# Attention's filling phase: two bias sums, one score step and the number of identity products moved

## The reference, cut to what matters

```
x = x + 0.5 * ffn(layernorm(x))          # shared SwiGLU plus one of 8 experts per token
x = x + attention(layernorm(x))          # the layer that the change touches
x = x + 0.5 * ffn(layernorm(x))
```

```
k, q, v = x @ Wk, x @ Wq / 4, x @ Wv          (per head)
s1 = softmax(q  @ k_l^T)     512 x 64
s2 = softmax(q_l @ k_l^T)     64 x 64
s3 = softmax(q_l @ k^T)       64 x 512
out = s1 @ (pinv(s2) @ (s3 @ v)) @ Wo + bo     (pinv: 6 steps of an iteration of matmuls)
```

## Time and profile before

| | |
|---|---|
| time, median of 3 runs | 1135.99 us (1130.5 to 1139.51) |
| the profiled execution | 1137.43 us |
| its span | 1135.5 us |
| PE busy | 1096.2 us, 97% of the span |
| DVE busy | 764.8 us, 67% |
| ACT busy | 582.7 us, 51% |
| POOL busy | 550.8 us, 49% |
| mean granted PE clock | 0.992 |
| busy of 46 us from 384 us on | PE 39.55, DVE 34.24, ACT 23.85, POOL 27.54 us, clock 0.93 |
| busy of 330 us from 430 us on | PE 313.21, DVE 258.77, ACT 173.72, POOL 131.49 us, clock 0.99 |

### The profile page before, as it was taken

How to read it: one execution, slowest core, us unless ns; L and a number is a source line. 1 busy time by engine, 2 the same in 40 slices (tenths; PEclk the granted TensorE clock), 3 DMA queues, 4 the chain that set the end, 5 groups by cost and what they waited for, 6 DMA issues and landing times.

```text
span 1135.5 us, 30299 instructions
## 1 busy us (share of the span) xinstructions
PE 1096.2 (97%) x11410; PEld 891.7 (79%) x11411; DVE 764.8 (67%) x1411; ACT 582.7 (51%) x961; POOL 550.8 (49%) x764
## 2 busy tenths in 40 slices
PE   8999999999999889999999999989999999999997
PEld 6788888888888767677777777768888888888886
DVE  5736656767677487868878878755447477677674
ACT  4344336666666345555555555243433256666663
POOL 5720644676666553444543541327202726566664
PEclk8999999999999989999999999999999999999999
DMA  7273134222211220000000000105241232122220
GB/s 259 74 292 117 37 116 173 66 67 71 66 61 45 65 89 3 3 3 3 3 3 3 3 3 3 39 3 212 101 152 38 102 140 68 62 67 62 71 65 14
DMA packets 39472, 80.25 MB, mean 71 GB/s; under 512 B 6452, under 2 KB 31159, under 8 KB 38336
## 3 DMA queue, kind: packets, MB, share of 16 engines
q1 hardware_dynamic: 27568, 52.94, 12.9%
q0 software_dynamic: 11232, 25.20, 7.1%
q10 hardware_dynamic: 560, 0.52, 0.1%
HBM read 57.13 MB, written 27.00 MB: 74 GB/s over the span
## 4 chain that ended last, share of the span: by engine, by line
PE 80%; DVE 11%; ACT 4%; issue 2%; POOL 1%; DMA 1%; ACTq 0%; DVEq 0%; SPq 0%; POOLq 0%
PE PS L1851 19%; PE PS L1765 13%; PE PS L1865 12%; PE PS L1781 8%; PE PS L1858 3%; PE PS L1939 3%; PE PS L1696 2%; DVE A_NM L801 2%; PE PS L2059 2%; PE PS L1799 2%; PE PS L2072 2%; DVE A_NM L808 1%; ACT XNT L1272 1%; PE PS L1792 1%; PE PS L2010 1%
## 5 line engine op out<-in xcount | busy, mean ns | idle before, releaser
L1851 PE MATMUL PS<-WHL,XGH 128*128 128x512 f32 x624 | 217.5, 430 | 0.6 <-DVE WHL L682 0.6
L1865 PE MATMUL PS<-WD,XNT 128*128 x624 | 149.5, 382 | 1.5 <-ACT XNT L1191 1.5
L703 DVE SCALAR_TENSOR_TENSOR XNT<-PS,SCORES,XNT 128x512 f32<-128x512 f32 x78 | 58.6, 751 | 117.4 <-PE PS L1851 117.4
L1599 POOL TENSOR_TENSOR A_W<-A_XC,CB 128x256 f32<-128x256 f32 x86 | 61.7, 737 | 151.4 <-DVE A_XC L906 151.4
L1186 ACT ACTIVATE XNT<-PS,SCORES 128x512 f32<-128x512 f32 x78 | 53.8, 690 | 145.2 <-PE PS L1851 145.0
L1851 PEld LDWEIGHTS PS<-WHL,XGH 128*128 128x128 f32 x624 | 111.4, 189 | 18.8 <-DVE WHL L682 1.1
L1865 PEld LDWEIGHTS PS<-WD,XNT 128*128 128x128 f32 x624 | 112.6, 190 | 15.6 <-issue 2.0
L1506 POOL DMA_INDIRECT X<-xs_dram,WHO x78 | 96.5, 1238 | 57.6 <-issue 23.1
L1851 PE MATMUL PS<-WHL,XGL 128*128 128x512 f32 x312 | 123.2, 395 | 0.0
L1500 POOL TENSOR_SCALAR XNT<-WD 128x128 f32<-128x128 f32 x64 | 52.4, 838 | 128.9 <-DVE WD L576 128.9
L1781 PE MATMUL PS<-SDH,HHL 128*128 128x256 f32 x512 | 104.0, 287 | 1.7 <-DVE X L616 1.3
(11 more groups left out here) (280 smaller groups left out, 2555.1 us busy)
## 6 DMA issues: line engine op xcount, KB each, us to landing
xs_dram<-WG SPq DMA_DIRECT2D x16, 512.0 KB, 3.0
WU<-in_r_up SPq DMA_DIRECT2D x2, 4096.0 KB, 14.3
shared_dram<-X SPq DMA_DIRECT2D x16, 512.0 KB, 2.9
WG<-in_r_gate SPq DMA_DIRECT2D x2, 4096.0 KB, 16.7
WD<-in_r_down SPq DMA_DIRECT2D x4, 2048.0 KB, 8.2
X<-in_x SPq DMA_DIRECT2D x7, 512.0 KB, 9.6
X<-mid_dram SPq DMA_DIRECT2D x7, 512.0 KB, 3.9
X<-xs_dram,WHO POOLq DMA_INDIRECT x78, 3.0
```

What stands on the lines that cost most here:

```text
L703: dve.scalar_tensor_tensor(B["RH"][:, u * F:(u + 1) * F], banks[3 + u][:], score(t), B["RS"][:, u * F:(u + 1) * F], ALU.mult, ALU.mult).th ...
L1599: pool.tensor_tensor(B["W"][:].rearrange("p (a m) -> p a m", m=M)[:, part, :], B["XC"][b % 2][:].rearrange("p (a w) -> p a w", w=XW)[:, pa ...
L1851: ins = pe.matmul(banks[bank][:], tok, w[:, k * F:(k + 1) * F], start=(k == 0 and i == 0), stop=(k == KD - 1 and i == 2))
L1865: ins = pe.matmul(banks[7][:, 0:D], B["HT"][:, u * F + f * P:u * F + (f + 1) * P], B["WD"][:, bass.ds(ex * (KF * D) + f * D, D)], start=(f ...
```

## The change

On POOL, `s2_normalise(0)` moves ahead of the first two bias sums. On PE, 8 in place of 3 identity products stand behind the transposes of batch 1, and the second step of the first softmax's scores stands directly behind the first Q projection of batch 1, ahead of the third softmax's transposed scores.

```diff
@@ attention_pool
             batch_root(1)
             batch_normalise(1)
+            s2_normalise(0)
             add_bias(0)
             add_bias(1)
-            s2_normalise(0)
             batch_root(2)
             batch_normalise(2)
             chain_w(0, 0)
@@ attention_tensor
             turn(1, 0)
             turn(1, 1)
-            fill(1, 3)
+            fill(1, 8)
             pe.wait_ge(att["s3m"], count("s3m", 0, 4))
             turn_nm3(0)
@@
             first_s1_max(0)
             pe.wait_ge(att["xtl"], count("xtl", 1, 2))
             project_qk(1, 0)
+            pe.wait_ge(att["s1m"], count("s1m", 0, 1))
+            first_s1_max(1)
             pe.wait_ge(s_picks, 5)
             pe.wait_ge(att["s2s"], count("s2s", 0, 1))
             s3_turned(0, 0)
-            pe.wait_ge(att["s1m"], count("s1m", 0, 1))
-            first_s1_max(1)
             project_qk(1, 1)
             pe.wait_ge(att["s1m"], count("s1m", 0, 2))
             first_s1_max(2)
```

## The result

The change makes the kernel a little slower: 1139.53 us (median of 20 runs) against 1134.26 for the kernel before (20 runs), a ratio of 1.0045 with an interval (here and below of 95%) from 1.0033 to 1.0057, or 5.1 us. The forecast was 1133.5 us and a gain of 2.45: wrong in its sign, and the time lies 1.5 us above its range. The profiled execution after took 1140.97 us, with a span of 1139.0.

What follows compares the result with a forecast made beforehand. Bound: a DVE, PE, DVE path in attention's filling, with keys held by POOL's bias sum. A 4.65 us gain less a 2.2 us hold gave 2.45, so 1133.5 us from the median of 1135.99; range 1128.5 to 1138.

Steps and rivals of the forecast that it cites:

- What bounds the kernel now: Start of attention: POOL's bias sum holds DVE's keys about 2.2 us, PE idles and its clock halves for 7 us.
- Five more identity products: PE before the third softmax's transpose: products cost up to 0.8 us, transpose at 406.1, still 1.36 us earlier than before.
- The moved score step: PE in attention's filling: DVE's 2.60 us gap goes, second maximum starts 4.65 us earlier; this part worth 0.7 to DVE.
- Bias sums at their new place: POOL beside lines 764 to 767: second sum holds line 767 for 2.2 us, cutting the gain from 4.65 to 2.45.
- Rival C: Attention's filling: PE stands 2.2 us for row sums, clock falls for 7 us, net 0.65 slower, 1136.6 us; chance 0.16.
- POOL's later work: POOL after the bias sums: W ready at 424.3, covered by 3.6 or 1.4 us before PE wants it.
- ACT's exponentials: Third softmax on ACT: start at 411.6, some 1.1 us later than otherwise, but covered by PE's work; counted as nothing.
- The upper end of the range: Whole kernel: cases span 1131.5 to 1136.6 us, a median strays 2 to 3 us around each, upper end 1138.

Runs made afterwards that it cites:

- e8: Kernel before with the moved score step, and POOL's first bias sum waiting for the semaphore of the keys of line 786; ratio 0.9989 to the kernel before.
- e12: Same edit as e8, measured again with more rounds: moved score step, first bias sum waiting for the keys; ratio 0.9990 to the kernel before.
- e6_pad: Kernel before with five more identity products (ten PE instructions) in the warm-up at attention's opening; ratio 1.0014 to the kernel before.
- e10: The change with its first two bias sums behind the first batch's chain weights 1 and 3, and 11 for 16 warm-up products; ratio 0.9998 to the kernel before.
- e4: The change with its first two bias sums moved out of the filling, behind the chain's second and fourth W of batch 0; ratio 1.0015 to the kernel before.
- e7: The whole change with five products fewer (11 for 16) in the warm-up at attention's opening; ratio 1.0017 to the kernel before.
- e2_step: Kernel before with only PE's moved score step, POOL's order and the 3 identity products as before; ratio 0.9999 to the kernel before.
- e0_before: Kernel before, unchanged, profiled a second time in one run; filling 28.1 us and loop 325.3 us, no ratio.
- e1: Kernel before with only the POOL part: the second softmax's normalisation ahead of the two bias sums; ratio 1.0033 to the kernel before.
- e11: The change without its five more identity products (3 for 8), bias sums and score step moved; ratio 1.0018 to the kernel before.
- e9_split_bias: The whole change with POOL's first two bias sums each written as four operations of 128x256; ratio 1.0029 to the kernel before.
- e3: Kernel before with only the five more identity products (8 for 3) behind the transposes of batch 1; ratio 1.0018 to the kernel before.

## Why the prediction was wrong, step by step

- **What bounds the kernel now: failed.** "So POOL's sum held DVE's two-operand product for about 2.2 us" was right of that execution. The step from it to the kernel was not: an order decided by 0.08 us was taken as fixed. In four of five traces with this POOL order the keys come first and take 0.48 to 0.49. The half clock of the earlier trace rows belongs to the same exception. The forecast priced the gain against the profiled execution and subtracted it from the median of the runs, most of which, going by e8 and e12, did not have these 31.3 - 28.1 = 3.2 us to gain.
- **Five more identity products: the cost beside them right, the cost behind them missed.** The products' own end and the transpose came within 0.1 us of the forecast (7.0 us behind the first scores; forecast 406.1 - 399.0 = 7.1). "Behind 430 us every engine keeps its order, so the gain is carried to the end" was false: the order is kept, but ten more instructions move every later one on in PE's stream, and PE stops at new places: 2.2 us there by the traces, and in sum 1.6 to 3.2 by the ratios of e6_pad, e10 against e4, and after against e7.
- **The moved score step: right in the trace.** The gap of 2.60 us is gone, the second maximum starts right behind the reciprocal (413.03 behind 412.81), and e2_step's filling is 1.9 us shorter than e0_before's, with PE not waiting at L2025 and no fall of the clock. In time it shows as 0.9999 (interval 0.9986 to 1.0012), which leaves room for a gain of up to 1.6 us; why it is less than 1.9 is open.
- **Bias sums at their new place: right.** A hold of 2.2 us on one of lines 764 to 767 was forecast; it was 2.41, 2.16, 2.18 and 2.41 for 0.17 of work in the four kernels that have the unsplit sums there (after, e1, e7, e11). It falls on 764, 765 or 767 as they happen to meet the handover, and is there in all four. By the Trainium skill's page "SBUF — State Buffer", section "Who interferes with whom", a DVE tensor_scalar in a two-port mode and a POOL instruction exclude each other for the whole instruction: four traces agree on the length of the hold, and so does e9_split_bias with 0.77 at most beside pieces of 0.70. Which mode DVE was in, no row says.
- **Rival C: under-rated at 0.16.** The standstill of 2.1 to 3.3 us brought the half clock in e1, e7 and e11, and the 1.6 us of e9 did too; of the traces with the bias sums at the new place, only after escaped. The filling then takes 31.2 to 31.7 us. With eight products it is 31.7 in e7 against 26.6 with neither hold nor fall (e4), with three 31.2 in e11 against 26.2 (e2): 5.0 to 5.1 more. The hold is 2.2 of that (28.8 - 26.6), the fall the rest, about 3 as forecast. Even the 1.27 us before L2025 in e0_before, e3 and e6 was followed by a shorter fall (clock 0.93 over 406 to 430), where the earlier trace rows had suggested that 1.28 is safe. The step removes that one.
- **POOL's later work, ACT's exponentials: right**, no new wait there shows up in the filling.
- **The upper end of the range: too low by the prediction's own rule.** Its cases end at 1136.6, and a median that strays by 2 to 3 us around them reaches 1138.6 to 1139.6, not 1138.

In sum, against e0_before as the usual kernel before: in the traces the moved step gains 1.9 us, the products cost 0.6 at the transpose, the hold takes 2.2 and with a fall of the clock about 5, the new stops take 2.2. That is between -1.9 + 0.6 + 2.2 + 2.2 = 3.1 and -1.9 + 0.6 + 5.1 + 2.2 = 6.0; measured 5.1 (3.7 to 6.5). How often the clock falls in the runs without a trace is known only through their mean clocks, so the shares of hold and fall within this stay open.

## What to carry to other kernels

A long stall that hangs on which of two engines comes first by 0.1 or 0.2 us may be a coin toss of that run, not a property of the kernel: look for the same row in a second execution before you price its removal. When an exclusive wait is moved, list the short operations at the new place, for each can be held for up to a whole piece of the other engine; cutting the sums in four shortened the hold only from 2.2 to 1.6 us here, because three operations then waited in a row. And instructions added to a long straight stream can cost at places far behind them: test an edit once more with the same number taken out elsewhere ahead of the loop.

## What the runs showed of the hardware that was not expected

- PE stops of 0.3 to 1.3 us in the middle of a group of products, without a releaser. Two places, at about 545 and 675 us, have one in all five traces with ten more PE instructions ahead and in none of the nine others. Other stops come and go between runs of one kernel: in e0_before a group of eight at L2010 is broken (below), which in the profiled kernel before takes 1.03 us unbroken. PE of e0_before:

```profile
659.15 1.02 PE L2010 MATMUL PS<-A_QT,X 32*128 32x512 f32 x2
660.57 1.13 PE L2010 MATMUL PS<-A_QT,X 32*128 32x512 f32 x6 [0.40 <-issue]
```

- The same standstill of 2.14 to 2.21 us was followed by the half clock in two kernels (e7, e11) and not in a third (after). One of 1.27 us was followed by a shorter fall in e0_before (window of e0_before, columns as above), and one of 1.28 was not before:

```profile
417.00:420.00 3.00, 3.00 (x14) 1.40 (x16) 1.72 (x4) 0.91 (x2) 2.20 (x9) 0.60 0.00 0
```

- A DVE operation on 128x4 elements, 0.17 us of work, took up to 2.41 us beside POOL's sum of 2.4. The other way round, a POOL operation of that size took 0.48 in place of 0.20 beside a DVE product of 0.42 us.
